# A DLRM interaction tower: one chunk of a layer moved ahead of the last transposes, the last small loads shared anew, and a wait before each gather

## The reference

```
e = stack([tbl_f[ids[:, f]] for f in range(27)], axis=1)        # 2048 x 27 x 128
x = einsum('bfd,bgd->bfg', e, e)[lower triangle]                # 2048 x 351
h = concatenate([bottom, x, bottom], axis=1)                    # 2048 x 607
h = maximum(h @ W_top1 + b_top1, 0)                             # 512 wide
h = maximum(h @ W_top2 + b_top2, 0)                             # 256 wide
y = h @ W_top3                                                  # 1 wide
```

## Time and profile before

| | us |
|---|---|
| median of 3 runs | 378.94 (378.78 to 379.65) |
| the profiled execution, its own time | 377.31 |
| its span, from the first to the last instruction | 375.5 |

### The profile page before, as it was taken

How to read it: one execution, slowest core, us unless ns; L and a number is a source line. 1 busy time by engine, 2 the same in 40 slices (tenths; PEclk the granted TensorE clock), 3 DMA queues, 4 the chain that set the end, 5 groups by cost and what they waited for, 6 DMA issues and landing times.

```text
span 375.5 us, 10311 instructions
## 1 busy us (share of the span) xinstructions
PE 338.1 (90%) x4321; PEld 326.6 (87%) x4321; DVE 247.9 (66%) x332; ACT 145.9 (39%) x280; POOL 267.5 (71%) x292
## 2 busy tenths in 40 slices
PE   0567869998999999999999989998999989997996
PEld 0456759997999999999999989998999989997985
DVE  2699997993699466953698176944598276952051
ACT  1466765615222443155313532145313522155202
POOL 6777777777777777777777777777777777775710
PEclk9998999999999999999999999999999999999999
DMA  7998874336443643345343643355243533323310
GB/s 153 232 223 242 261 209 131 86 81 163 149 121 77 193 114 89 84 100 194 78 108 68 192 108 91 83 136 166 61 111 73 192 107 96 81 60 82 63 16 1
DMA packets 47058, 45.76 MB, mean 122 GB/s; under 512 B 33033, under 2 KB 35930, under 8 KB 47013
## 3 DMA queue, kind: packets, MB, share of 16 engines
q1 hardware_dynamic: 36050, 26.88, 27.3%
q0 software_dynamic: 9184, 17.93, 18.2%
q10 hardware_dynamic: 1779, 0.30, 0.4%
HBM read 39.52 MB, written 5.55 MB: 120 GB/s over the span
## 4 chain that ended last, share of the span: by engine, by line
PE 77%; DMA 7%; DVE 6%; POOL 3%; issue 3%; ACT 3%; SPq 1%
PE work L465 41%; PE gram L492 10%; PE work L477 6%; PE work L518 4%; PE work L519 4%; PE work L520 4%; DMA raw_lo<-in_tbl 4%; DVE onehot L625 3%; DMA emb<-in_tbl,ids_all 3%; POOL emb L433 3%; PE work L535 2%; PE work L537 2%; PE work L536 2%; DVE tab_lo L610 2%; SPq L355 1%
## 5 line engine op out<-in xcount | busy, mean ns | idle before, releaser
L433 POOL DMA_INDIRECT emb<-in_tbl,ids_all x272 | 258.3, 950 | 84.0 <-issue 78.0
L625 DVE TENSOR_TENSOR onehot<-ids_bc,row_idf 125x1024 fp32r<-125x1024 int32 (+2 forms) x232 | 198.8, 920 | 35.7 <-PE work L465 29.4
L465 PE MATMUL work<-onehot,tab_hi 125*128 125x256 f32 x672 | 168.8, 291 | 24.1 <-ACT tab_hi L734 13.7
L465 PE MATMUL work<-onehot,tab_lo 125*128 125x256 f32 x672 | 165.2, 286 | 0.0
L465 PEld LDWEIGHTS work<-onehot,tab_hi 125*128 125x128 f32 x672 | 130.5, 194 | 30.0 <-issue 14.4
L465 PEld LDWEIGHTS work<-onehot,tab_lo 125*128 125x128 f32 x672 | 130.8, 195 | 0.0
L776 ACT COPY embT<-work 128x512 f32<-128x512 f32 (+1 forms) x36 | 26.9, 799 | 103.4 <-PE work L465 103.4
L492 PE MATMUL gram<-embT 128*54 128x52 f32 x1920 | 51.6, 214 | 2.3 <-ACT embT L595 2.1
L492 PEld LDWEIGHTS gram<-embT 128*54 128x54 f32 x1920 | 49.6, 130 | 4.6 <-ACT embT L595 1.3
L477 PE MATMUL work<-ident,emb 128*128 128x128 f32 x272 | 35.4, 275 | 4.7 <-DMA emb<-in_tbl,ids_all 4.7
L783 ACT COPY inter<-gram 118x416 f32<-118x416 f32 x64 | 32.4, 508 | 16.6 <-PE gram L492 14.6
(11 more groups left out here) (55 smaller groups left out, 225.5 us busy)
## 6 DMA issues: line engine op xcount, KB each, us to landing
ids_bc<-in_sel_ids SPq DMA_DIRECT2D x14, 512.0 KB, 4.4
grams<-inter SPq DMA_DIRECT2D x62, 84.5 KB
emb<-in_tbl,ids_all POOLq DMA_INDIRECT x272
ids_bc<-in_sel_ids SPq DMA_DIRECT2D x11, 256.0 KB, 9.5
misc<-in_tbl SPq DMA_DIRECT2D x3, 448.0 KB
inter<-in_tbl SPq DMA_DIRECT2D x3, 448.0 KB
raw_w<-in_W_top SPq DMA_DIRECT2D x4, 256.0 KB, 7.2
misc<-in_bottom SPq DMA_DIRECT2D x8, 128.0 KB
```

The source lines that it names most:

```text
L433: pool.indirect_dma_start(out=emb[:, t % TILE_SLOTS, f, :], out_offset=None, in_=gather_tables[f], in_offset=bass.IndirectOffsetOnAxis(ap= ...
L465: mm = nc.tensor.matmul(out, part[0:k, CHUNK_AT[f] + c, :], onehot[0:k, at % RING, i * HALF:(i + 1) * HALF], start=(c == 0 and i % 2 == 0 ...
L625: nc.vector.tensor_tensor(onehot[0:k, at % RING, 0:width], ids_bc[0:k, four[0]:four[-1] + 1, :].rearrange("p i n -> p (i n)"), row_idf[0:k ...
```

## The change

In the last half, the `bottom` chunk of `mlp1(6)` (12 matmuls) stands before `rows(15)`, and the other three chunks stay behind `products(15)`. Its two banks are claimed there too, so `rows(15)` has three banks left: groups 3 and 4 take those of groups 0 and 1 again. `products` now waits for the banks of selections and transposes alone. The last 28 loads are dealt 11, 11 and 6 to SP, ScalarE and POOL. And before each gather from table 5 of tile 4 on POOL waits, beside its old waits, for a step of TensorE (`behind`); the first two gathers of tile 6 are left out, so 197 gathers of the 272 have such a wait.

```diff
-    POOL_PACKS = PACKS[5::6]
+    POOL_PACKS = PACKS[2::5]
...
+    def claim(*key, n=None):
+        if n is None:
+            n = use["next"] = use.get("next", -1) + 1
         use[key] = (n % BANKS, used[n % BANKS])
         used[n % BANKS] += 1
+        if key[0] in ("select", "rows"):
+            embedded[n % BANKS] = used[n % BANKS]
...
     def take_gram(t):
-        upto["gram", t] = list(used)
+        upto["gram", t] = list(embedded)
...
-        take_rows(2 * h + 1)
+        if h + 1 == HALVES:
+            claim_mlp1(h - 1)
+            take_rows(2 * h + 1, range(BANKS - 2))
+            first = use["next"] - (BANKS - 3)
+            for g in range(BANKS - 2, NGR):
+                claim("rows", 2 * h + 1, g, n=first + g - (BANKS - 2))
+                signal("rows", 2 * h + 1, g)
+            use["next"] = first + BANKS - 1
+        else:
+            take_rows(2 * h + 1)
...
-    take_mlp(HALVES - 2, "mlp1")
+    signal_mlp1(HALVES - 2)
...
+            def behind(h, n):
+
+                even, odd = 2 * h, 2 * h + 1
+                if n < 3:
+                    pool.wait_ge(grammed, even * GRAMS + (1, 3, 4)[n])
+                elif n < 7:
+                    is_filled(pool, "rows", odd, (1, 4, 4, 4)[n - 3])
+                elif n < 10:
+                    is_filled(pool, "mlp1", h - 1, n // 9)
+                elif n < 13:
+                    pool.wait_ge(grammed, odd * GRAMS + (1, 3, 4)[n - 10])
+                elif n < 25:
+                    pool.wait_ge(onehot_used, OH_AT[h + 1] + (1, 2, 4, 5, 6, 7, 9, 10, 11, 12, 14, 15)[n - 13])
+                elif n < 27:
+                    is_filled(pool, "rows", even + 2, (0, 3)[n - 25])
+                elif n < 31:
+                    pool.wait_ge(onehot_used, OH_AT[h + 1] + (18, 20, 23, 25)[n - 27])
+                elif n == 31:
+                    is_filled(pool, "bottom", h + 1)
+                else:
+                    is_filled(pool, "mlp2", h - 1, n - 32)
...
                     for f in features:
+                        n = t % TILE_SLOTS * NGA + f
+                        if t >= 8 or t >= 6 and n >= 2:
+                            behind(t // 2 - (1 if n >= 2 else 2), (n - 2) % (2 * NGA))
+                        elif t >= 4 and n >= 5:
+                            behind(1, n - 5)
                         pool.indirect_dma_start(
...
                 mlp3(h - 2)
+                if h == HALVES - 1:
+                    mlp1(h - 1, X_ORDER[:1])
                 rows(2 * h + 1, range(NGR))
...
-            mlp1(HALVES - 2)
+            mlp1(HALVES - 2, X_ORDER[1:])
             mlp1(HALVES - 1, X_ORDER[:1])
             mlp2(HALVES - 2)
```

More of the change, by code:

```diff
@@ L116, in dlrm_tower @@
     SET_START = [four[0] for four, _, _ in TWOS]
-    use, fill, used, upto = {}, {}, [0] * BANKS, {}
-    def claim(*key):
-        n = use["next"] = use.get("next", -1) + 1
+    use, fill, used, upto, embedded = {}, {}, [0] * BANKS, {}, [0] * BANKS
+    def claim(*key, n=None):
+        if n is None:
+            n = use["next"] = use.get("next", -1) + 1
         use[key] = (n % BANKS, used[n % BANKS])
         used[n % BANKS] += 1
+        if key[0] in ("select", "rows"):
+            embedded[n % BANKS] = used[n % BANKS]
     def signal(*key):
```

## The result

The changed kernel takes 375.83 us (median of 12 executions, 375.42 to 377.02), and the kernel before takes 378.36 us beside it (12 executions, 376.90 to 379.65): a ratio of 0.9933, 95% interval 0.9917 to 0.9950. It is 0.7% faster: 2.5 us where 1.3 were forecast. The forecast started from the median of three executions of the kernel before, 378.94 us. The profiled execution took 376.00 us, its span is 374.2 us. Against the profiled execution of the kernel before that is 1.31 us less, and the forecast for it was 376.02. So the forecast met the pair of traces and missed the pair of medians, and the question is what lies in the executions that the first trace doesn't show.

The account below looks back on a forecast made before the run. POOL's gathers bound the kernel until the last lands at 345.85 us, then TensorE does. 377.31 - 1.44 + 0.15 = 376.02 us profiled; median 378.94 - 1.29 = 377.65 us, other terms 0; 8-in-10 range 377.0 to 379.2.

Parts of the forecast that it names:

- POOL sets the pace, the last gather the end: Gathers start 1.25 us apart without a break; the last lands at 345.85 us, and TensorE runs nearly closed from there.
- The moved chunk: 1.44 us out of the tail, 0.15 lost ahead of it: 12 matmuls leave the stretch behind `products(15)` for the idle time at `rows(15)`; bank waits and matmul switch lose 0.15 us.
- the sum: Whole kernel: 377.31 - 1.44 + 0.15 = 376.02 us profiled; 378.94 - 1.29 = 377.65 us for the median.
- The median of the runs is 1.63 us above the profiled execution before, and I keep that.: Step from profiled to timed runs: the kernel before's 1.63 us difference is kept, giving 377.65 us, 0.34% faster.
- Dealing 11, 11, 6: Last loads on SP, ScalarE and POOL: both ends lie inside the slack, 0; up to 0.4 us if slack were gone.
- the third cast would not wait: VectorE's rounding of packed products in the tail: no wait ahead of the third; at least 1.0 us of slack left.
- The 197 waits cost nothing and hold nothing: POOL's waits ahead of gathers: all have passed, closest margin 1.67 us; 0, bounds -0.4 to +9.9 us.
- costly waits: Rival at POOL's 0.30 us gap: passed waits cost time, slower than before from 10.4 ns each; chance 0.13.
- late steps: Rival at tile 6: a TensorE step comes after its gather and holds POOL; with 4 us, 380.0 us; chance 0.03.
- the gather at 30.59: POOL gather said to have two waits, the ids and the transposes, yet the usual 0.30 us gap; supports free waits.
- the 57 doubled waits: Gathers waiting for both transposes and a step; at 0.05 us each, 377.65 + 2.9 = 380.5 us.
- slow gathers: Rival on POOL: the waits take away its few slow gathers, about 0.4 us together, giving 377.25 us; chance 0.05.

Follow-up runs that it names:

- sitting h: Beside the kernel before (378.09 us): the moved chunk alone, without POOL's waits or new dealing, 376.34 us; chunk in both places, without the waits, 377.80 us.

## Why the prediction was right in its trace and wrong in its time

1. *POOL sets the pace, the last gather the end.* Right. The last gather starts at 342.97 in the kernel after, as before (342.87), and the gathers are 1.25 us apart in both.
2. *The moved chunk: 1.44 us out of the tail, 0.15 lost ahead of it.* Right in the trace: `rows(15)` at 344.62 (344.54 forecast), products at 347.70 (347.75), end of the span at 374.2 (374.2), and 1.46 us by the two kernels of sitting h. This is the 1.3 us of the sum.
3. *"The median of the runs is 1.63 us above the profiled execution before, and I keep that."* This is the step that failed. The prediction carried the 1.63 us over as a constant, without a reason for it. The kernel after has nothing of it: its median, 375.83, lies 0.17 us below its profiled execution. Two things were in the 1.63. One belongs to the kernel before: two more traces of it, 1.6 us above the first, have a fallen clock behind the idle time ahead of `products(15)`, for 1.56 and 1.58 us, and the change takes away most of that idle time. The prediction even had the two idle times on record, 1.25 and 1.05 us, and priced them only by their length. The other is chance: the three executions behind the median of 378.94 were all of the slower kind (378.78 to 379.65), which is 21 of 58 later on, while the medians of the kernel before are 378.36 (with these three among its 12), 377.90 and 378.09, 0.6 to 1.1 us above the trace. How much of these 0.6 to 1.1 us the fallen clock makes is known only by the estimate above, 0.57 us.
4. *Dealing 11, 11, 6.* Right, 0 within what the runs can tell. The forecast that the third cast would not wait was wrong (0.61 us), and the slack that it counted on took the wait.
5. *The 197 waits cost nothing and hold nothing.* Right where the kernel before takes 378 us (1.0009). The rivals of costly waits and late steps didn't happen. One reading behind it was wrong, though: the gather at 30.59 is the sixth of tile 1 and has no wait at all (line 431 starts with the third tile). The first one with two waits, the ids and the transposes, is the first of tile 2, at 45.56, and its gap is 0.30 us too, so the argument holds. The 2.9 to 5.7 us that the prediction estimated for the 57 doubled waits didn't appear either: the waits alone take at most 1.1 us more (a ratio of up to 1.0030). Where the kernel before takes 630 us they are the largest gain of the change. The first trace shows nothing of that, and the prediction had no term for it.
6. *The range.* Of 377.0 to 379.2, the low end came from slow gathers alone. It should have held the case in which the 1.63 us go too: 376.0. The measured 375.83 is below that by less than the 0.2 us that the prediction gave the measurement.

## What to carry to other kernels

Idle time of TensorE can cost more than its length when it stands close ahead of dense matmuls: here the granted clock fell behind it in some executions, for 1.57 us. A filler that removes the gap may gain even if it is as long as the gap; in this case that gain alone was 0.29 us by the median and not clear of noise. When a median lies clearly above the traced execution, the difference is a term of its own. Ask first whether the median is of enough executions, then what makes the difference and whether the change touches that, before carrying it over. And a kernel that lets one engine run far ahead should also be timed in another sitting: a wait that has always passed in one was worth a fifth of the time in another.

## What was not expected of the hardware

- The same program took 378 us and 630 us in different sittings, on chips of the same number (4: 378.09 and 629.47; 14: 377.90 and 633.17).
- In the condition of 630 us a gather on POOL still takes 0.95 us and its gap is 0.30, while single products of TensorE come 0.70 us apart (249.43, 250.13) where the first trace has 3.41 us for 128, and 118 take 4.51 us as soon as POOL stands still.
- The granted clock fell behind idle times of 1.21 and 1.05 us in one trace of the kernel before and of 1.32 and 1.05 in another, and did not fall behind 1.25 and 1.05 us in the first, nor behind 1.17 and 1.05 with the waits alone. The same program has both.
